# Four-chosen experts: two pairs' weights spread by TensorE, low weight parts made by GpSimd, chunk 1 prepared between the first units

## The chip, the core and the metric

The kernel runs on one core of a Trainium2 chip. The metric is the device time of one execution in microseconds (us). The core's engines run beside each other, each with its own order of instructions: TensorE (PE; its weight loads are PEld), VectorE (DVE), ScalarE (ACT), GpSimd (POOL) and SyncE (SP), which issues DMAs. They wait for each other through semaphores.

## The reference

A stack of eight blocks on x of 2048 tokens by 128 features: softmax attention, two-chosen experts, a selective scan, two-chosen experts again, linear attention, four-chosen experts, gated linear attention, and four-chosen experts again. The change is in the function for the four-chosen experts, which is built twice. Cut to what matters:

```python
def _gate(x_flat, gate_w, e_bias):
    scores = sigmoid(x_flat @ gate_w.T)                  # 16 experts in 4 groups
    scores_for_choice = scores + e_bias
    # the sum of the best 2 of a group rates it; the best 2 groups stay; of their experts the best 4
    topk_weight = scores at the 4 chosen; weight / (weight.sum + 1e-20) * 2.5
x = x + _L1_attn_a_ref(_layernorm(x), ...)
x = x + _L1_ffn_ref(_layernorm(x), ...)                  # four-chosen experts, first stage
x = x + _L1_attn_b_ref(_layernorm(x), ...)
x = x + _L1_ffn_ref(_layernorm(x), ...)                  # four-chosen experts, second stage
#   with, in _L1_ffn_ref:
g = einsum('th,eih->eti', x, gate_proj); u = einsum('th,eih->eti', x, up_proj)
expert_out = einsum('eti,ehi->eth', silu(g) * u, down_proj)
y = sum over the chosen experts of topk_weight * expert_out
out = y + (silu(x @ shared_gate_w.T) * (x @ shared_up_w.T)) @ shared_down_w.T
```

## The kernel before

`experts_top4` (line 1883) works on 4 chunks (NC_) of 512 tokens (CH), each of 4 tiles (TPC) of 128. Work is laid out transposed: features on the partitions, tokens in the columns. The 16 experts have a hidden width of 64, so two share the 128 partitions: 8 pairs. With the shared expert, unit 0, a chunk has 9 units (UNITS); units are numbered g = 9c + u over the chunks, 36 in all (LAST).

A unit goes through four steps. `up(g)` (line 1994) is six matmuls on TensorE into two PSUM banks, gate and up: products in float32r are made exact enough by splitting weights and rows into a high and a low part, three matmuls for each bank (`SplitRows.matmul`, lines 120 to 122). `silu(g)` (line 2058) on ScalarE makes the gate. `multiply(g)` (line 2103) on VectorE multiplies the gate with the routing weights, spread over the partitions (line 2110, increments `scaled`), and then with the up bank (line 2116, increments `hidden_done`). `down(g)` (line 2006) is four matmuls of 128 columns (eight records, as float32 takes two for each) that add into the bank DOWN over all units of a chunk; `add(c)` adds the bank to x. Three sets of buffers (SETS) let up(g+3) start when hidden(g) is done.

The high part of the weights is rounded by ScalarE (line 2083, four instructions for two pairs each), the low part is subtracted by VectorE (`cut_weights`, line 2130, after multiply(0)); `up` waits for it on line 2002. A chunk's rows are prepared by `stat_rows` and `norm_rows` on VectorE (lines 162 to 168 and 183) with GpSimd's `root` between them (line 177), `turn` on TensorE (line 192), `copy_turned` on ScalarE (lines 200 and 202) and `cut_rows` on VectorE (line 210). Routing is `score` (TensorE, line 1975, into bank DOWN for chunk 0, SCRATCH for others), `tanh` (ScalarE), and `rate_groups`, `rank_groups`, `find_best`, `select` and `weigh` on VectorE, 28 short instructions in a chain (lines 2143 to 2200). The weights are turned by `turn_probs` (line 1985) into bank SCRATCH and copied by `copy_probs` (line 2066) to probsT, 16 rows of 512. SyncE stores them to DRAM (line 1946) and then loads each expert's row back into 64 partitions, two loads for a pair, into a ring of six tiles (line 1953).

Order on the engines is written by hand. TensorE (lines 2021 to 2047): turn(0), score(0), up(0), turn_probs(0), up(1), up(2); then for each unit g: turn(1) and score(1) at g = 1, down(g), up(g+3); from chunk 1 on turn_probs at u = 7, the next turn at u = 8, score at u = 0. ScalarE: round the shared weight, copies of chunk 0, tanh(0), silu(0), the four roundings, copy_probs(0), silu(1) to silu(3), the copies of chunk 1, tanh(1). VectorE: routing of chunk 0, multiply(0), cut_weights, then stat_rows(1), norm_rows(1), cut_rows(1), and only then multiply(1); the routing of the next chunk is put behind multiply of units 1 to 5 (one part each), statistics, normalising and cutting of the chunk after it behind units 6, 7 and 8.

## Time and profile before

| | us |
|---|---|
| median of 3 runs | 1628.84 (1627.59 to 1629.21) |
| the profiled execution | 1628.38 |
| its span | 1626.7 |
| TensorE busy in the span | 1485.5 (91%) |
| VectorE busy in the span | 1360.6 (84%) |
| first four-chosen stage, about | 1321 to 1435 |
| second four-chosen stage, about | 1512 to 1625 |

The profile is of one execution. A timeline row has the start in us from the span's start, the busy time, the engine, the line of the kernel, the operation, output<-inputs, shapes and the number of instructions merged; in brackets the idle time before it and what released it. TensorE's granted clock is given as a share of 2.4 GHz.

### The profile page before, as it was taken

Reading aid. Unit: us, or ns where it says so; the run is one execution under the profiler, and the core shown is the slowest. Engines: PE = TensorE matmul, PEld = TensorE weight load, DVE = VectorE, ACT = ScalarE, POOL = GpSimd, SP = SyncE. Lnnn points to the kernel's source line nnn. Section 1 sums busy time; section 2 is a strip of 40 time slices with the busy share of each in tenths; the row PEclk is TensorE's granted clock in tenths of the full one; section 3 lists DMA queues with packets and bytes.
Section 4 is the critical chain, followed back from the end, with each engine's and each line's share of the span. In section 5 each row is a group of like instructions: output and inputs, shape, how many; then the busy total and the mean of one; then the engine's idle time right before and its main releaser. Section 6 shows DMA issues by size and latency. Waiting matters only on the chain. (4 is left out here: it accounts for less than half of the span.)

```text
span 1626.7 us, 27667 instructions
## 1 busy us (share of the span) xinstructions
PE 1485.5 (91%) x10314; PEld 771.6 (47%) x10314; DVE 1360.6 (84%) x2455; ACT 936.1 (58%) x1751; POOL 295.8 (18%) x352
## 2 busy tenths in 40 slices
PE   7999999999999999799997898877999869989698
PEld 2122222222222222488862333324888748869587
DVE  7999999999999997476747999997767658787686
ACT  3189999999999999532236666653322332222232
POOL 4200000000000000000016878872000200020000
PEclk8599999999999999899999999999999979999799
DMA  3341100000000011000002222120000002300123
GB/s 108 118 141 31 34 31 25 25 25 25 25 24 25 32 42 33 1 1 1 1 1 72 73 66 69 66 71 4 1 1 1 1 19 88 106 1 1 53 84 101
DMA packets 41329, 66.15 MB, mean 41 GB/s; under 512 B 11444, under 2 KB 18661, under 8 KB 40490
## 3 DMA queue, kind: packets, MB, share of 16 engines
q1 hardware_dynamic: 41194, 64.37, 12.9%
q8 instruction: 82, 1.34, 0.3%
q14 instruction: 53, 0.43, 0.1%
HBM read 56.68 MB, written 6.75 MB: 39 GB/s over the span
## 5 line engine op out<-in xcount | busy, mean ns | idle before, releaser
L874 DVE TENSOR_REDUCE row_max<-ps 128x1 f32<-128x1024 f32 x512 | 585.1, 1213 | 16.5 <-PE ps L659 16.2
L780 ACT ACTIVATE probs<-ps 128x512 f32<-128x512 f32 x944 | 505.6, 596 | 57.1 <-PE ps L674 40.6
L659 PE MATMUL ps<-k_stack,q_stack 48*128 48x512 bf16 x1024 | 323.7, 402 | 8.4 <-DMA k_stack<-parts 2.7
L600 PE MATMUL ps<-probs,v_head 128*16 128x256 f32 (+1 forms) x3800 | 313.5, 402 | 6.3 <-issue 6.3
L674 PE MATMUL ps<-q_stack,k_stack 51*128 51x512 bf16 x944 | 286.9, 385 | 3.4 <-DMA q_stack<-max_dram 2.7
L1400 PE MATMUL ps<-s_hc,ident 128*128 128x512 f32 x256 | 139.0, 628 | 47.9 <-DVE s_hc L1673 42.8
L1053 ACT ACTIVATE x_gate<-ps 128x512 f32<-128x512 f32 x128 | 76.4, 598 | 184.5 <-PE ps L122 184.4
L659 PEld LDWEIGHTS ps<-k_stack,q_stack 48*128 48x128 bf16 x1024 | 60.1, 95 | 253.7 <-DVE row_max L874 234.6
L1325 POOL TENSOR_TENSOR s_dbx<-s_dx,s_b_rows 128x512 f32<-128x512 f32 x128 | 159.4, 1271 | 35.2 <-DVE s_h L1664 34.7
L1664 DVE TENSOR_TENSOR_SCAN s_h<-ps,s_state,s_dbx 128x512 f32<-128x512 f32 x128 | 156.8, 1266 | 4.5 <-POOL s_dbx L1325 2.8
L600 PEld LDWEIGHTS ps<-probs,v_head 128*16 128x16 f32 x3800 | 62.6, 94 | 201.5 <-issue 100.8
L1555 ACT ACTIVATE ps<-s_delta,s_a_neg 128x512 f32<-128x512 f32 x128 | 87.3, 689 | 77.7 <-DVE s_h L1664 76.7
L1090 DVE TENSOR_TENSOR x_hidden<-x_gate,ps 128x512 f32<-128x512 f32 x128 | 87.1, 686 | 53.4 <-PE ps L122 42.8
L1022 PE MATMUL ps<-w_w,x_hidden 128*128 128x128 f32 x1024 | 124.9, 275 | 0.0
L1022 PEld LDWEIGHTS ps<-w_w,x_hidden 128*128 128x128 f32 x1024 | 122.7, 192 | 3.6
L2063 ACT ACTIVATE y_gate<-ps 128x512 f32<-128x512 f32 (+1 forms) x72 | 43.0, 597 | 118.9 <-PE ps L122 118.9
L120 PE MATMUL ps<-x_x_high,x_w_high 128*128 128x512 f32 x256 | 107.6, 420 | 1.0 <-DVE x_hidden L1090 1.0
L122 PE MATMUL ps<-x_x_low,x_w_high 128*128 128x512 f32 x256 | 102.3, 400 | 0.0
L1400 PEld LDWEIGHTS ps<-s_hc,ident 128*128 128x128 f32 x256 | 45.6, 195 | 117.1 <-DVE s_hc L1673 87.6
L121 PE MATMUL ps<-x_x_high,x_w_low 128*128 128x512 f32 x256 | 101.1, 395 | 0.0
L1101 DVE SCALAR_TENSOR_TENSOR x_res<-ps,x_probs,x_res 128x128 f32<-128x128 f32 x256 | 72.1, 344 | 34.7 <-PE ps L1022 34.4
L1673 DVE TENSOR_TENSOR s_hc<-s_h,ps 128x512 f32<-128x512 f32 x128 | 80.9, 670 | 1.0 <-PE ps L1400 1.0
(346 smaller groups left out, 1953.6 us busy)
## 6 DMA issues: line engine op xcount, KB each, us to landing
s_b_rows<-s_b_dram SPq DMA_DIRECT2D x64, 256.0 KB, 3.2
y_spread<-y_probs_dram SPq DMA_DIRECT2D x128, 128.0 KB, 3.0
q_stack<-q_parts_dram SPq DMA_DIRECT2D x30, 96.0 KB
k_stack<-k_parts_dram SPq DMA_DIRECT2D x30, 96.0 KB
w_w<-w_dram SPq DMA_DIRECT2D x1, 2048.0 KB, 8.3
q_stack<-q_parts_dram SPq DMA_DIRECT2D x30, 64.0 KB
k_stack<-k_parts_dram SPq DMA_DIRECT2D x30, 64.0 KB
o_dram<-o_sb SPq DMA_DIRECT2D x60, 32.0 KB
```

Of the source, the lines that this page charges most:

```text
L120: nc.tensor.matmul(bank, self.w_high[:, u, cols], self.x_high[:, chunk], start=True, stop=False)
L121: nc.tensor.matmul(bank, self.w_low[:, u, cols], self.x_high[:, chunk], start=False, stop=False)
L122: return nc.tensor.matmul(bank, self.w_high[:, u, cols], self.x_low[:, chunk], start=False, stop=True)
L600: last = nc.tensor.matmul(core.ps[32 * c:32 * c + VROWS, O_BANK, cut], v_head[buf][:, kt, :], probs[:, m % RING, c * CH:(c + 1) * CH][:, cut],
L659: last = nc.tensor.matmul(core.ps[:, 2 * b + r, :], qst[buf][0:KROWS, u * P:(u + 1) * P], kst[buf][0:KROWS, key:key + CH], start=True, sto ...
L674: nc.tensor.matmul(core.ps[:, S_BANK + n % S_RING, :], kst[buf][HALF:ROWS, kt * P:(kt + 1) * P], qst[buf][HALF:ROWS, c * CH:(c + 1) * CH], ...
L780: nc.scalar.activation(probs[:, us % RING, c * CH:(c + 1) * CH], core.ps[:, S_BANK + n % S_RING, :], ACT.Exp).then_inc(exp_done, 1)
L874: nc.vector.tensor_reduce(mx[:, head % 2, u, b:b + 1], core.ps[:, 2 * b:2 * b + 2, :], mybir.AxisListType.XY, ALU.max).then_inc(max_done, 1)
L1022: last = nc.tensor.matmul(core.ps[:, DOWN + n % 2, k * P:(k + 1) * P], hidden[n % 2][:, half, k * P:(k + 1) * P], w["w3"][:, e, half, :], ...
L1325: nc.gpsimd.tensor_tensor(dbx[u % RING][:], dx[c % 2][d][:], b_rows[g % RING][:], ALU.mult).then_inc(dbx_done, 1)
L1400: nc.tensor.matmul(core.ps[:, Y_BANK + d, :], core.ident[:], hc[d][:], start=s == 0, stop=s == DS - 1).then_inc(summed, 1)
L1664: nc.vector.tensor_tensor_scan(out=h[g % 2][:, d, :], data0=core.ps[:, A_BANKS[d], :], data1=dbx[u % RING][:], initial=state[:, s, d:d + 1 ...
```

## The change

Four things in `experts_top4`, for chunk 0 alone or for the preparation of chunk 1:

- The routing weights of pairs 0 and 1 of chunk 0 no longer come through DRAM. `spread_rows` has TensorE multiply probsT with a column of the identity, repeated 64 times, once for each half of the partitions, into bank SCRATCH (pair 0) and bank DOWN (pair 1); multiply(1) and multiply(2) read them there. SyncE loads pairs 2 to 7. down(0), which writes DOWN, waits until multiply(2) has read it.
- The low parts of the 8 pairs' weights are subtracted by GpSimd; ScalarE rounds two groups ahead of silu(0) and two behind it.
- TensorE's order becomes turn(0), score(0), up(0), up(1), up(2), turn_probs(0), the two spreads, up(3), down(0), turn(1), down(1), up(4), score(1), down(2) and so on. ScalarE copies probs after silu(2), the turned rows of chunk 1 after silu(3), and makes tanh(1) after silu(4).
- VectorE: statistics of chunk 1 follow multiply(0), normalising follows multiply(1), the cut multiply(2); the routing of chunk 1 follows units 4 (two parts), 5 (two parts) and 6. Later chunks are as before.

```diff
--- before.py
+++ after.py
@@ -1887,7 +1887,7 @@
     PAIRS = E1 // 2
     UNITS = PAIRS + 1
     PG = E1 // GROUPS
-    SETS, P_RING = 3, 6
+    SETS, P_RING, BY_PE = 3, 6, 2
     DOWN, SCRATCH = 2 * SETS, 2 * SETS + 1
     LAST = NC_ * UNITS
     with ExitStack() as ctx:
@@ -1919,6 +1919,8 @@
         scored = core.sem(f"{tag}_scored")
         tanh_done = core.sem(f"{tag}_tanh")
         probs_ready = core.sem(f"{tag}_probs_ready")
+        rows_spread = core.sem(f"{tag}_rows_spread")
+        w_rest = core.sem(f"{tag}_w_rest")
         probs_turned = core.sem(f"{tag}_probs_turned")
         probs_copied = core.sem(f"{tag}_probs_copied")
         probs_stored = core.sem(f"{tag}_probs_stored")
@@ -1945,7 +1947,7 @@
                 sp.wait_ge(probs_copied, c + 1)
                 sp.dma_start(pd[c], probsT[:]).then_inc(probs_stored, 16)
                 sp.wait_ge(probs_stored, 16 * (c + 1))
-                for pair in range(PAIRS):
+                for pair in range(0 if c else BY_PE, PAIRS):
                     m = c * PAIRS + pair
                     if m >= P_RING:
                         sp.wait_ge(scaled, m - P_RING + 1)
@@ -1962,6 +1964,12 @@
         def _(pool):
             if following:
                 following.set_power(pool)
+            for i in range(PAIRS // 2):
+                pool.wait_ge(cut.w_rounded, i + 2)
+                nc.gpsimd.tensor_tensor(cut.w_low[:, 1 + 2 * i:3 + 2 * i, :],
+                                        w["w_up1"][:, 2 * i:2 * i + 2, :, :].rearrange("p u k d -> p u (k d)"),
+                                        cut.w_high[:, 1 + 2 * i:3 + 2 * i, :].bitcast(F32),
+                                        ALU.subtract).then_inc(w_rest, 1)
             ln.root(pool, 1)
             for g in range(LAST):
                 c, u = g // UNITS, g % UNITS
@@ -1999,7 +2007,10 @@
                 if u == 0:
                     pe.wait_ge(ln.x_cut, c + 1)
                 if c == 0:
-                    pe.wait_ge(cut.w_cut, 1 + (u + 1) // 2)
+                    if u:
+                        pe.wait_ge(w_rest, (u + 1) // 2)
+                    else:
+                        pe.wait_ge(cut.w_cut, 1)
                 for k in range(2):
                     cut.matmul(core.ps[:, 2 * (g % SETS) + k, :], u, slice(k * P, (k + 1) * P), cols).then_inc(up_done, 1)
 
@@ -2007,7 +2018,7 @@
                 c, u = g // UNITS, g % UNITS
                 pe.wait_ge(hidden_done, g + 1)
                 if u == 0 and c == 0:
-                    pe.wait_ge(tanh_done, 1)
+                    pe.wait_ge(scaled, BY_PE)
                 elif u == 0:
                     pe.wait_ge(added, c)
                 for k in range(TPC):
@@ -2018,18 +2029,34 @@
                                             stop=u == UNITS - 1 and k == TPC - 1)
                 last.then_inc(down_done, 1)
 
+            def spread_rows(pair):
+                if pair == 0:
+                    pe.wait_ge(probs_copied, 1)
+                else:
+                    pe.wait_ge(tanh_done, 1)
+                for i in range(2):
+                    e = 2 * pair + i
+                    last = nc.tensor.matmul(core.ps[i * I1:(i + 1) * I1, (SCRATCH, DOWN)[pair], :],
+                                            core.ident[0:E1, e:e + 1].to_broadcast([E1, I1]), probsT[:],
+                                            start=True, stop=True)
+                last.then_inc(rows_spread, 1)
+
             core.loaded(pe, "gate1", "w_down1", "sh_down")
             ln.turn(pe, 0)
             score(0)
-            up(0)
+            for g in range(SETS):
+                up(g)
             turn_probs(0)
-            for g in range(1, SETS):
-                up(g)
+            for pair in range(BY_PE):
+                spread_rows(pair)
             for g in range(LAST):
                 c, u = g // UNITS, g % UNITS
+                if g == 0:
+                    up(SETS)
                 if g == 1:
-                    pe.wait_ge(probs_copied, 1)
+                    pe.wait_ge(scaled, 1)
                     ln.turn(pe, 1)
+                if g == 2:
                     score(1)
                 if u == 7 and c + 1 < NC_:
                     turn_probs(c + 1)
@@ -2043,7 +2070,7 @@
                         pe.wait_ge(probs_copied, NC_)
                     following.turn(pe, u - 5)
                 down(g)
-                if g + SETS < LAST:
+                if g and g + SETS < LAST:
                     up(g + SETS)
 
         @block.scalar
@@ -2075,17 +2102,25 @@
             ln.copy_turned(act, 0)
             core.act_line.after(act, nc.scalar.activation(warm[:], core.one[:], ACT.Silu))
             tanh(0)
+
+            def round_weights(i):
+                nc.scalar.copy(cut.w_high[:, 1 + 2 * i:3 + 2 * i, :],
+                               w["w_up1"][:, 2 * i:2 * i + 2, :, :].rearrange("p u k d -> p u (k d)")).then_inc(
+                                   cut.w_rounded, 1)
+
+            round_weights(0)
+            round_weights(1)
             for g in range(LAST):
                 c, u = g // UNITS, g % UNITS
                 silu(g)
                 if g == 0:
-                    for i in range(PAIRS // 2):
-                        nc.scalar.copy(cut.w_high[:, 1 + 2 * i:3 + 2 * i, :],
-                                       w["w_up1"][:, 2 * i:2 * i + 2, :, :].rearrange("p u k d -> p u (k d)")).then_inc(
-                                           cut.w_rounded, 1)
+                    round_weights(2)
+                    round_weights(3)
+                if g == SETS - 1:
                     copy_probs(0)
                 if g == SETS:
                     ln.copy_turned(act, 1)
+                if g == SETS + 1:
                     tanh(1)
                 if u == 0 and c:
                     copy_probs(c)
@@ -2106,9 +2141,13 @@
                 dve.wait_ge(gate_done, g + 1)
                 if u:
                     m = c * PAIRS + u - 1
-                    dve.wait_ge(spread_loaded[m % P_RING], 32 * (m // P_RING + 1))
-                    nc.vector.tensor_tensor(gate[g % SETS][:], gate[g % SETS][:], spread[m % P_RING][:],
-                                            ALU.mult).then_inc(scaled, 1)
+                    if m < BY_PE:
+                        dve.wait_ge(rows_spread, m + 1)
+                        weights = core.ps[:, (SCRATCH, DOWN)[m], :]
+                    else:
+                        dve.wait_ge(spread_loaded[m % P_RING], 32 * (m // P_RING + (m % P_RING >= BY_PE)))
+                        weights = spread[m % P_RING][:]
+                    nc.vector.tensor_tensor(gate[g % SETS][:], gate[g % SETS][:], weights, ALU.mult).then_inc(scaled, 1)
                     dve.wait_ge(scaled, m + 1)
                 dve.wait_ge(up_done, 2 * g + 2)
                 if g >= SETS:
@@ -2126,14 +2165,6 @@
                 dve.wait_ge(cut.w_rounded, 1)
                 nc.vector.tensor_tensor(cut.w_low[:, 0, :], w["sh_up"][:].rearrange("p k d -> p (k d)"),
                                         cut.w_high[:, 0, :].bitcast(F32), ALU.subtract).then_inc(cut.w_cut, 1)
-
-            def cut_weights():
-                for i in range(PAIRS // 2):
-                    dve.wait_ge(cut.w_rounded, i + 2)
-                    nc.vector.tensor_tensor(cut.w_low[:, 1 + 2 * i:3 + 2 * i, :],
-                                            w["w_up1"][:, 2 * i:2 * i + 2, :, :].rearrange("p u k d -> p u (k d)"),
-                                            cut.w_high[:, 1 + 2 * i:3 + 2 * i, :].bitcast(F32),
-                                            ALU.subtract).then_inc(cut.w_cut, 1)
 
             def rate_groups(c):
                 part = slice(c * TPC, (c + 1) * TPC)
@@ -2210,17 +2241,28 @@
             select(0)
             weigh(0)
             multiply(0)
-            cut_weights()
             ln.stat_rows(dve, 1)
-            ln.norm_rows(dve, 1)
-            ln.cut_rows(dve, 1)
             for g in range(LAST):
                 c, u = g // UNITS, g % UNITS
                 if g:
                     multiply(g)
                 if u == 0 and c:
                     add(c - 1)
-                if c + 1 < NC_:
+                if c == 0:
+                    if u == 1:
+                        ln.norm_rows(dve, 1)
+                    elif u == 2:
+                        ln.cut_rows(dve, 1)
+                    elif u == 4:
+                        rate_groups(1)
+                        rank_groups(1)
+                    elif u == 5:
+                        find_best(1)
+                        select(1)
+                    elif u == 6:
+                        dve.wait_ge(probs_ready, 1)
+                        weigh(1)
+                elif c + 1 < NC_:
                     if u == 1:
                         rate_groups(c + 1)
                     elif u == 2:
```

## Rows read from the trace of the kernel before

**Rows 1.** The page, busy time of each engine.

```profile
PE 1485.5 (91%) x10314; PEld 771.6 (47%) x10314; DVE 1360.6 (84%) x2455; ACT 936.1 (58%) x1751; POOL 295.8 (18%) x352
```

**Rows 2.** Windows, first stage: length, busy (instructions) by engine, clock, DMA share, GB/s.

```profile
1321.00:1336.00 15.00, 8.94 (x27) 6.43 (x28) 10.61 (x45) 6.93 (x13) 0.09 (x1) 0.50 0.02 4
1336.00:1343.00 7.00, 5.09 (x26) 3.75 (x25) 2.77 (x13) 2.35 (x5) 1.01 (x1) 0.98 0.47 133
1343.00:1350.30 7.30, 7.23 (x29) 6.68 (x30) 5.91 (x21) 0.82 (x2) 0.00 (x0) 0.53 0.53 158
1350.30:1367.40 17.10, 17.02 (x109) 14.87 (x108) 14.53 (x45) 5.87 (x11) 1.39 (x1) 1.00 0.11 29
```

**Rows 3.** Timeline, all engines, 1325 to 1328.

```profile
1325.27 0.77 PE L120 MATMUL ps<-y_x_high,y_w_high 128*128 128x512 f32 x1
...
1325.89 0.19 DVE L2143 TENSOR_SCALAR y_scores<-y_scores 128x64 f32<-128x64 f32 x1 [1.68 <-ACT y_scores L2054]
...
1327.43 2.16 ACT L2083 CAST y_w_high<-w_w_up 128x512 fp32r<-128x512 f32 x4
...
1327.55 0.63 PE L122 MATMUL ps<-y_x_low,y_w_high 128*128 128x512 f32 x1
```

**Rows 4.** Timeline, all engines, 1332 to 1337.

```profile
1332.33 0.22 DVE L2200 TENSOR_TENSOR y_probs<-y_gt,y_total 128x64 f32<-128x64 f32 x1
...
1332.61 1.02 PE L1990 MATMUL ps<-ident,y_probs 128*16 128x128 f32 x4 [4.43 <-DVE y_probs L2200]
...
1333.07 2.48 DVE L2133 TENSOR_TENSOR y_w_low<-w_w_up,y_w_high 128x512 fp32r<-128x512 f32 x4
...
1333.67 0.57 ACT L2070 COPY y_probsT<-ps 16x512 f32<-16x512 f32 x1 [4.08 <-PE ps L1990]
...
1333.80 0.80 PE L120 MATMUL ps<-y_x_high,y_w_high 128*128 128x512 f32 x1 [0.17 <-DVE y_w_low L2133]
...
1336.94 11.63 SPq L1953 DMA_DIRECT2D y_spread<-y_probs_dram  x16
```

**Rows 5.** Timeline, the preparation of chunk 1, 1336 to 1343.

```profile
1336.79 0.17 DVE L168 TENSOR_SCALAR ln_m_veps<-ln_m_mv 128x4 f32<-128x4 f32 x1
...
1337.11 1.01 POOL L177 TENSOR_TENSOR ln_m_rstd<-ln_m_veps,ln_m_power 128x4 f32<-128x4 f32 x1 [16.01 <-DVE ln_m_veps L168]
...
1338.15 1.12 DVE L183 TENSOR_SCALAR xn<-x_res,ln_m_mv,ln_m_rstd 128x128 f32<-128x128 f32 x4 [1.19 <-POOL ln_m_rstd L177]
...
1340.49 0.60 PE L192 MATMUL ps<-ident,xn 128*128 128x128 f32 x4
...
1342.23 0.69 DVE L210 TENSOR_TENSOR y_x_low<-ps,y_x_high 128x512 fp32r<-128x512 f32 x1 [2.97 <-ACT xnT L202]
...
1342.84 0.68 DVE L2110 TENSOR_TENSOR y_gate<-y_gate,y_spread 128x512 f32<-128x512 f32 x1
```

**Rows 6.** Timeline, VectorE and TensorE in full stride, and down(9).

```profile
1354.64 0.69 DVE L2110 TENSOR_TENSOR y_gate<-y_gate,y_spread 128x512 f32<-128x512 f32 x1
...
1354.89 0.48 PE L120 MATMUL ps<-y_x_high,y_w_high 128*128 128x512 f32 x1
...
1355.98 0.22 DVE L2196 TENSOR_TENSOR y_gt<-y_scores,y_sel 128x64 f32<-128x64 f32 x1
...
1357.17 0.48 PE L120 MATMUL ps<-y_x_high,y_w_high 128*128 128x512 f32 x1
...
1367.40 1.13 PE L2015 MATMUL ps<-w_sh_down,y_hidden 64*128 64x128 f32 x8
```

**Rows 7.** Lines and timeline elsewhere: prices of operations like the new ones.

```profile
L1325 POOL TENSOR_TENSOR s_dbx<-s_dx,s_b_rows 128x512 f32<-128x512 f32 x128 | 159.4, 1271 | 35.2 <-DVE s_h L1664 34.7
...
1359.93 1.39 POOL L177 TENSOR_TENSOR ln_m_rstd<-ln_m_veps,ln_m_power 128x4 f32<-128x4 f32 x1 [21.82 <-DVE ln_m_veps L168]
...
1436.45 2.81 PE L2382 MATMUL ps<-xnT,w_W_in 128*128 128x512 f32 x6 [1.52 <-PEq L1893]
...
499.63 0.63 PE L600 MATMUL ps<-probs,v_head 128*16 128x256 f32 x8
```

## The prediction

> **What bounds the kernel now.** I read the page first: TensorE is busy for 91% of the span [rows 1], so a gain has to come from a place where it is idle or slow. The table by windows over the first four-chosen stage shows such a place [rows 2]. In 1321 to 1336 TensorE is busy for 8.9 of 15 us, at a granted clock of 0.50 (1.2 GHz); in 1343 to 1350.3 it is busy all the time but at 0.53; from 1350.3 it is full, at 1.00 (2.4 GHz). The timeline says why. TensorE ends up(0) at 1328.0 and then waits until 1332.6 for the routing weights of chunk 0, because turn_probs(0) stands ahead of up(1) in its order; VectorE works on those weights without a pause from 1325.9 to 1332.55 [rows 3, 4]. The four weight subtractions follow (1333.1 to 1335.55), and up(1) waits for the first of them until 1333.8 [rows 4]. Then VectorE prepares the rows of chunk 1 before multiply(1): statistics to 1336.96, waiting for GpSimd's root, 1.12 us of normalising, and 2.97 us waiting for TensorE's turn and ScalarE's copies; the cut is at 1342.23, and multiply(1) starts at 1342.84 [rows 5]. From unit 4 on TensorE is the bound: 2.28 us a unit against 1.34 us of multiplying and 1.1 to 1.6 us of routing on VectorE [rows 6]. So the stage has a start set by VectorE's order and a long part set by TensorE. The yardstick is down(9), the first product of chunk 1, at 1367.40 [rows 6]: behind it both kernels issue the same work. The second four-chosen stage repeats these rows 191.3 us later, so what one stage gains counts twice.
>
> **Part by part.** *Low parts to GpSimd.* VectorE loses 4 instructions, 2.48 us [rows 4]. GpSimd gets 4 subtractions of 128x512; its tensor_tensor of that size takes 1.27 us [rows 7], 5.1 us in all. ScalarE now rounds two groups ahead of silu(0): it is free when tanh has released VectorE at 1325.9, and takes 0.54 us for each [rows 3], so the first low part exists at 1325.9 + 0.54 + 1.27 = 1327.7, before up(0) ends at 1328.0, and all four by 1331.5, ahead of the root for chunk 1 that is queued behind them. silu(0) moves by at most 0.1 us; nobody waits, since hidden(0) comes after the routing.
>
> *up(1), up(2) ahead of turn_probs(0).* They fill the idle 4.6 us. At the low clock each takes 2.56 us (six at 0.43) [rows 3] and up(2) ends at 1333.1, 0.5 us after the routing weights; if the clock rises on the way, at 1331 to 1332, and nothing is late. In the kernel before the clock rose at 1336, 3.4 us after TensorE took up steady work at 1332.6 [rows 2, 4]; here steady work starts at 1325.3, so I take a rise at about 1329 to 1332.
>
> *Weights of pairs 0 and 1 by TensorE.* Four loads of sixteen leave SyncE's queue; pair 2 is then the first, and its load, issued at about 1336.5, is in long before it is wanted. The store still goes ahead of it. In exchange: turn_probs at 1332.6, which takes 0.63 us to ScalarE's start at the full clock (1.06 at the low one [rows 4]), the copy 0.57 [rows 4], and two matmuls of 512 f32 columns with 64 output rows each. The nearest row: six records of 512 f32 columns, two to a matmul, in 2.81 us [rows 7], so 0.9 us for one. Whether the two halves of the partitions run together decides between 0.9 and 1.8 us. The row nearest to it is the value product of attention, four column blocks side by side: eight records (four matmuls) of 256 f32 columns in 0.63 us [rows 7], where four in turn would take 1.8 by the 0.9 for 512 columns; I take together. At the full clock the pair's weights are then ready at 1332.6 + 0.63 + 0.6 + 1.1 = 1334.95. At the low clock this is 1336.3, or 1338 with the halves in turn.
>
> The Trainium skill, "TensorEngine Tiling (Array Packing)", Key Properties, says that tiles run in parallel and that a change of tiling mode drains TensorE. The attention row agrees with the first half; no row here separates out a drain, and the sum has none.
>
> *Chunk 1 between the units.* VectorE: multiply(0) and statistics end at 1334.55; multiply(1) 1334.95 to 1336.3 (1.34 [rows 6]); normalising to 1337.4; the scaling of multiply(2) ends at 1338.05. There is one new wait: down(0) now waits for it, because its bank holds the weights of pair 1, and turn(1) is queued behind down(0). Meanwhile TensorE has done the second spread and up(3), to 1337.2, and idles 0.9. down(0) 1.06 (taken from a unit's share, 2.28 less six times 0.23, and a little more for the wait ahead of it [rows 6]), turn(1) 0.6, ScalarE's two copies 1.1 (1341.1 to 1342.2 [rows 5]): cut_rows(1) at 1340.9 instead of 1342.23 [rows 5], and multiply(1) and (2) are already done. That is the gain: two units of VectorE work (2.7) and the low parts (2.5) leave the stretch between the weights and this point.
>
> From there VectorE is the bound to the end of chunk 0, since routing for chunk 1 now lies in units 4 to 6: cut 0.6, multiply(3) to (8) 6 x 1.34 = 8.0, routing 6.6 (1325.89 to 1332.55 [rows 3, 4]), statistics and normalising of chunk 2 1.4 + 1.1 [rows 5], and 1.4 us for GpSimd's root beside a multiply [rows 7], partly covered: 0.1. Sum 17.8, multiply(8) ends at 1359. TensorE is not late: its five units from 1344 take 11.4. It has up(11) done at 1361.4 (down(8) waits for multiply(8), then turn(2) and up(11) at 2.3), score(2) 1.04, and down(9) starts at about 1362.3, against 1367.40: 5.1 us.
>
> Off this I take 0.8: 0.3 for GpSimd delayed beside VectorE and 0.5 for a clock that may be low over part of the spread. That leaves 4.3 a stage, 8.6 in all. The profiled execution took 1628.4 (span 1626.7 and 1.7 around it), 0.4 below the median of 1628.8; its sum is 1619.8, and on the median it is 1620.2.
>
> **What isn't shown before.** GpSimd streaming while VectorE reads two SBUF tensors: GpSimd's 4-column root takes 1.39 us beside the two-tensor multiply, where it takes 1.01 without it [rows 5, 7], so GpSimd yields and VectorE's 0.69 doesn't change. Bounds: nothing (as beside the scan, 1.27), up to each low part doubled (10 us), which puts the root 2 us late. Whether VectorE's chain of 28 small instructions slows, no row shows: from 0 to the whole 5.1 us, if the two took turns. I take 0, as VectorE's row says. The Trainium skill, "GPSIMD Engine Reference", Key points, states that the two engines contend where VectorE has two SBUF inputs or a two-port mode, which nearly all these 28 have; by that rule alone the gain could be nil, as in the port case below.
>
> **Rivals.** *The clock is low over the spread.* TensorE idles about 1 us ahead of turn_probs and 0.6 behind it. Before, an idle stretch of 2 us at 1341 was followed by the low clock [rows 2]; the gaps here are shorter. Price: turn 0.43 and matmuls 0.9 at least, queue 0.5 and later waits 0.5 besides: 1.3 to 2.3 us of the 5.1. Taking 2.3 and the 0.3 for GpSimd, 2.5 is left: 1623.8.
> *Port.* GpSimd's and VectorE's streams stretch each other on the routing chain: 2 to 3 us in each stage, 1.8 left: 1625.2. Its extreme, 5.1, is no change: 1628.8.
> *Slower.* The spread runs at the low clock and its halves in turn, 3.4 us each: pair 0 at 1338, pair 1 at 1341.3, multiply(2)'s scaling at 1342.1, up(3) at the low clock to 1343.9, down(0) and turn(1) 2.8, copies 1.1: the cut at 1347.9 instead of 1340.9, and down(9) 7.0 later than in the sum and 0.4 more for units still at the low clock, at 1369.7, 2.3 late: 1633.4. It decides where up(3), down(0), turn(1) and the copies (6.5 in all) behind pair 1's weights reach 1340.9 + 5.1: from 1339.5 on. Against it: eight attention records side by side.
> *It does not do it.* The starting wait merely changes its name: down(0)'s new wait, or VectorE's compressed chunk-1 routing, costs what was won. The sum has 4 us in hand before this holds: 1628.8.
>
> **How the numbers follow.** Forecast case 55% (1618.0 to 1622.5), low clock 20% (up to 1624.9), port 12% (1623 to 1628.8), not done 6%, slower 7%. The low end is 5.5 us a stage with everything free: 1617.5. The high end takes in the low clock and half of the port case: 1626.5. A difference under 0.2% (3.3 us) can't be told from none in this kernel. Faster by more: 55 + 19 + 5 = 79%; within: 13%; slower: 8%.
>
> **What would show it.** Right: up(1) at 1328 directly behind up(0); pair 0's scaling at about 1335; cut_rows(1) at about 1341; down(9) at about 1362; GpSimd's four rows near 1.3 us; granted clock 1.0 from about 1331. Wrong: pair weights after 1336 (clock, or halves in turn); routing weights later than 1332.6 after the stage's start at 1321 (port); VectorE idle in units 4 to 8 while TensorE works (then the sum of chunk 0 is wrong).

## The result, and the profile after

The changed kernel takes 1633.44 us (median of 7 runs, 1631.58 to 1636.14) against 1628.87 for the kernel before (7 runs); the ratio is 1.0032, with a 95% interval of 1.0023 to 1.0041. It is slower by 0.3%, where the forecast was 0.5% faster. The page after:

```profile
span 1634.4 us, 27691 instructions
...
PE 1494.0 (91%) x10330; PEld 775.1 (47%) x10330; DVE 1364.5 (83%) x2447; ACT 936.6 (57%) x1751; POOL 305.9 (19%) x360
```

The profiled execution took 1636.14 us, the longest of the seven. Its first four-chosen stage begins 3.0 us later than before (first turn 1324.31, before 1321.29), in code that is the same up to there; so I count from the stage's first turn.

The windows that answer to [rows 2], from the stage's first turn on, cut at the end of the routing before (11.3 us), near the start of down(0) before (16; it is 16.6), the cut of chunk 1 before (21) and after (28). The columns are the same: length, busy time and instructions of PE, PEld, DVE, ACT and POOL, granted clock, DMA share, GB/s.

```profile
1324.30:1335.60 11.30, 9.31 (x30) 7.13 (x30) 7.56 (x16) 6.81 (x13) 5.08 (x4) 0.62 0.01 1
1335.60:1340.30 4.70, 0.41 (x3) 0.26 (x4) 4.18 (x22) 0.00 (x0) 0.00 (x0) 0.93 0.00 0
1340.30:1345.30 5.00, 4.34 (x12) 0.99 (x10) 3.06 (x14) 0.57 (x1) 1.01 (x1) 0.50 0.12 39
1345.30:1352.30 7.00, 7.00 (x25) 5.74 (x26) 2.08 (x6) 1.67 (x3) 0.00 (x0) 0.50 0.59 198
1352.30:1374.30 22.00, 21.22 (x133) 18.55 (x133) 19.00 (x63) 6.88 (x13) 1.39 (x1) 0.98 0.11 34
```

TensorE fills the first stretch as planned, and near its end, at 1332.8, its clock rises to 2.4 GHz. Then it is idle: busy for 0.4 of 4.7 us. From 1340.3 to 1352.3 it is busy almost throughout, at a granted clock of 0.50 (1.2 GHz). The timeline of the routing, after, shows what the idle stretch waits for:

```profile
1329.40 0.19 DVE L2178 TENSOR_TENSOR y_hi<-y_choice 128x32 f32<-128x32 f32 x1
1329.43 5.08 POOL L1969 TENSOR_TENSOR y_w_low<-w_w_up,y_w_high 128x512 fp32r<-128x512 f32 x4 [5.32 <-ACT y_w_high L2107]
1329.51 1.28 DVE L2179 TENSOR_TENSOR y_lo<-y_choice 128x32 f32<-128x32 f32 x1
...
1330.83 1.20 DVE L2180 TENSOR_TENSOR y_g_best<-y_hi 128x16 f32<-128x16 f32 x1
...
1331.95 0.16 DVE L2181 TENSOR_TENSOR y_g_next<-y_hi 128x16 f32<-128x16 f32 x1
1332.03 1.26 DVE L2182 TENSOR_TENSOR y_g_low<-y_lo 128x16 f32<-128x16 f32 x1
...
1333.33 1.21 DVE L2183 TENSOR_TENSOR y_g_next<-y_g_next,y_g_low 128x16 f32<-128x16 f32 x1
...
1334.58 0.17 DVE L2184 TENSOR_TENSOR y_g_best<-y_g_best,y_g_next 128x16 f32<-128x16 f32 x1
```

GpSimd's four subtractions run from 1329.43 to 1334.51, 1.27 us each, as [rows 7] had said. Beside each, one short VectorE instruction takes 1.2 to 1.3 us; the same lines take 0.17 to 0.18 us in every other chunk. L2181, which begins together with GpSimd's third, slips through in 0.16. The first instruction that starts after GpSimd is done takes 0.17 again. The chain from its first step to the routing weights takes 10.9 us (1328.91 to 1339.83) where it took 6.7 [rows 3, 4]. What follows, after:

```profile
1339.61 0.22 DVE L2231 TENSOR_TENSOR y_probs<-y_gt,y_total 128x64 f32<-128x64 f32 x1
...
1339.89 1.02 PE L1998 MATMUL ps<-ident,y_probs 128*16 128x128 f32 x4 [5.11 <-DVE y_probs L2231]
...
1340.95 0.57 ACT L2097 COPY y_probsT<-ps 16x512 f32<-16x512 f32 x1 [6.22 <-PE ps L1998]
...
1341.58 3.68 PE L2039 MATMUL ps<-y_probsT,ident 16*64 16x512 f32 x8 [0.66 <-ACT y_probsT L2097]
...
1343.66 0.69 DVE L2150 TENSOR_TENSOR y_gate<-y_gate,ps 128x512 f32<-128x512 f32 x1 [1.84 <-PE ps L2039]
...
1348.04 2.07 PE L2026 MATMUL ps<-w_sh_down,y_hidden 64*128 64x128 f32 x8
...
1352.30 0.69 DVE L210 TENSOR_TENSOR y_x_low<-ps,y_x_high 128x512 fp32r<-128x512 f32 x1 [4.88 <-ACT xnT L202]
...
1374.08 1.13 PE L2026 MATMUL ps<-w_sh_down,y_hidden 64*128 64x128 f32 x8
```

turn_probs(0) comes 5.1 us after TensorE's last work and at the low clock; the two spreads take 3.68 us, down(0) 2.07, where 1.06 was expected. The cut of chunk 1 is at 1352.30, 28.0 us after the first turn (before 20.9 [rows 5]). From there to down(9) it is 21.8 us, where the sum had 21.4. The second stage repeats the first: down(9) 49.96 after its first turn, 46.10 before the change.

This table gives the marks of the first four-chosen stage of every kernel, in us after its first turn, from the timelines; in brackets the second stage where it differs by over 0.3. "x before" is the ratio of the times.

| kernel | routing weights begin | multiply(1) | cut of chunk 1 | down(9) | x before |
|---|---|---|---|---|---|
| before | 11.0 | 21.6 | 20.9 | 46.1 | 1 |
| after | 15.3 | 19.4 | 28.0 | 49.8 | 1.0032 |
| e1, before with GpSimd's low parts | 14.4 | 24.7 | 24.1 | 49.2 | 1.0034 |
| e2, after, low parts in VectorE's gaps | 11.1 | 13.8 | 21.2 | 42.8 | 0.9945 |
| e3, after, GpSimd's behind the routing | 11.0 | 18.4 (18.8) | 24.5 (24.8) | 45.9 (46.3) | 0.9985 |
| e4, after, GpSimd's in halves | 15.0 | 19.1 (18.7) | 27.7 (27.3) | 49.5 | 1.0028 |
| e5, e2 with turn(1) first | 11.1 | 13.8 | 18.9 | 41.3 | 0.9933 |
| e6, e2 with idle filled | 11.1 | 13.8 | 20.5 (21.2) | 41.9 (42.8) | 0.9944 |
| e7, e2 without the spread | 11.1 | 17.8 | 22.1 | 44.7 | 0.9985 |
| e8, e5 with half of up(3) early | 11.1 | 14.0 | 18.3 | 42.6 (40.3) | 0.9931 |
| e9, after with idle filled | 15.3 | 18.1 | 24.7 | 46.2 | 0.9991 |
| e10, before with the gaps used | 11.1 | 18.9 | 18.3 | 43.5 | 0.9963 |

### The profile page after: what moved, and what is told of

Same layout as the page of the kernel before. It is cut to its first block and busy times, and to the rows that moved or that the text cites. A ratio compares the mean times of both kernels' runs of the same rounds, so it can differ in the third digit from the quotient of the medians.

```text
span 1634.4 us, 27691 instructions
## 1 busy us (share of the span) xinstructions
PE 1494.0 (91%) x10330; PEld 775.1 (47%) x10330; DVE 1364.5 (83%) x2447; ACT 936.6 (57%) x1751; POOL 305.9 (19%) x360
## 5 line engine op out<-in xcount | busy, mean ns | idle before, releaser
L1090 DVE TENSOR_TENSOR x_hidden<-x_gate,ps 128x512 f32<-128x512 f32 x128 | 87.2, 686 | 53.3 <-PE ps L122 42.8
L508 POOL TENSOR_TENSOR neg_max_parts<-neg_maxT,by_one 128x32 bf16<-128x32 f32 x16 | 4.0, 251 | 418.5 <-DVE neg_maxT L867 418.5
```

## The experiments

The theory after the result had two parts: P, GpSimd's streaming holds up VectorE's routing instructions, and K, the wait that this makes lets TensorE's clock fall, which stretches all that follows. The rival C was that the order and the clock alone are to blame.

**e1_low_by_gpsimd.** One part of the change alone, in the kernel before.

```diff
         def _(pool):
+            for i in range(PAIRS // 2):
+                pool.wait_ge(cut.w_rounded, i + 2)
+                nc.gpsimd.tensor_tensor(cut.w_low[...], w["w_up1"][...], cut.w_high[...], ALU.subtract).then_inc(w_rest, 1)
             ln.root(pool, 1)
...
             multiply(0)
-            cut_weights()
```

> The kernel before with one thing changed: the four subtractions of the low weight parts are GpSimd's instead of VectorE's (TensorE's order, the DRAM way of the routing weights and the preparation of chunk 1 stay). Theory P (port: while GpSimd's tensor_tensor streams, a VectorE instruction with two SBUF inputs waits for its end): some four of the short routing instructions take 1.2 to 1.3 us instead of 0.2, the routing weights of chunk 0 come 4 us later after the stage's first turn (15.3 instead of 11.3), and with 2.5 us of VectorE work gone that was not on the path the time is 8 us above before, 1636.5. Rival C (the changed kernel lost its time only to the clock and the new order): the short instructions keep 0.2 us and the time is 1628.5.

Measured: 1634.51 us, ratio 1.0034 (1.0022 to 1.0046); the routing weights 3.3 us late, down(9) 3.1. Timeline:

```profile
1328.80 0.22 DVE L2174 TENSOR_TENSOR y_g_beats<-y_g_beats,y_g_ties 128x64 f32<-128x64 f32 x1
1328.82 4.99 POOL L1968 TENSOR_TENSOR y_w_low<-w_w_up,y_w_high 128x512 fp32r<-128x512 f32 x4 [7.09 <-ACT y_w_high L2093]
1329.06 0.22 DVE L2175 TENSOR_REDUCE y_g_rank<-y_g_beats 128x16 f32<-128x64 f32 x1
1329.32 0.87 DVE L2177 TENSOR_SCALAR y_g_rank<-y_g_rank 128x16 f32<-128x16 f32 x1
1330.22 1.24 DVE L2181 TENSOR_TENSOR y_tmp_scores<-y_choice,y_g_rank 128x64 f32<-128x64 f32 x1
1331.49 0.41 DVE L2186 MAX8 y_top<-y_tmp_scores 128x8 f32<-128x16 f32 x4
1331.93 0.74 DVE L2189 TENSOR_TENSOR y_gt<-y_tmp_scores,y_top 128x64 f32<-128x64 f32 x1
1332.60 1.29 DVE L2190 TENSOR_TENSOR y_eq<-y_tmp_scores,y_top 128x64 f32<-128x64 f32 x1
```

P holds, C falls: this one edit costs as much as the whole change. The last two lines show best that it is a wait for the end of GpSimd's instruction: L2189 begins midway through GpSimd's third, which ends at 1332.59, and takes 0.74 us; L2190 meets the fourth almost whole and takes 1.29. Here other routing instructions are hit, those that happen to lie beside GpSimd's, so it is not a property of single lines. The four MAX8 (0.41 us together) and the reduction, each with one SBUF input, keep their time; tensor_tensor with two SBUF inputs and tensor_scalar don't. Less was lost than I expected (5.5 us, not 8): the weights are 3.3 us late in each stage, not 4.

**e2_low_in_vector_gaps.** The changed kernel with that part given back to VectorE, half of it ahead of the routing.

```diff
-                nc.gpsimd.tensor_tensor(cut.w_low[...], ...)            # all four
+            round_weights(0)                                            # ScalarE, before copy_turned(0)
+            round_weights(1)                                            # ScalarE, before tanh(0)
             cut_shared()
+            cut_pairs(0)
             ln.cut_rows(dve, 0)
+            cut_pairs(1)
             rate_groups(0)
...
             ln.stat_rows(dve, 1)
+            cut_pairs(2)                                                # cut_pairs(3) behind multiply(2)
```

> The changed kernel with the low parts taken from GpSimd again: ScalarE rounds two groups before tanh(0), VectorE subtracts pairs 0 to 3 in its two idle stretches ahead of the routing, pairs 4 to 7 behind the statistics of chunk 1 and behind multiply(2). All else of the change stays. Theory P: the routing weights come 11.3 us after the first turn again. If port and clock cost 4.3 and 4.1 us a stage, as the traces read, only the first goes: each stage is 0.6 us shorter than before, 1627.5. If the clock was low only because TensorE waited 5 us for the late weights, it stays at 2.4 GHz now and the blind forecast's sum holds: down(9) 46.1 - 5 = 41 us after the first turn, 1619. Rival C: no better than the changed kernel, 1633.

Measured: 1620.19 us, ratio 0.9945 (0.9933 to 0.9957). Timeline:

```profile
1333.26 1.93 PE L2033 MATMUL ps<-y_probsT,ident 16*64 16x512 f32 x8 [0.66 <-ACT y_probsT L2091]
...
1334.46 0.69 DVE L2143 TENSOR_TENSOR y_gate<-y_gate,ps 128x512 f32<-128x512 f32 x1
...
1337.64 2.04 PE L2020 MATMUL ps<-w_sh_down,y_hidden 64*128 64x128 f32 x8
...
1341.87 0.69 DVE L210 TENSOR_TENSOR y_x_low<-ps,y_x_high 128x512 fp32r<-128x512 f32 x1 [3.05 <-ACT xnT L202]
```

The two spreads take 1.93 us at 2.4 GHz, pair 0's weights are read 2.5 us after the routing's end (the forecast's term was 2.4). With the low parts in this place the change gains 0.55%; e10 below shows how much of it is the place. Not all of the clock came back: down(0) still takes 2.04, so the cut is at 21.2 and not at the forecast's 19.6.

**e3_low_after_routing.** GpSimd keeps the subtractions but starts them when the routing is done.

```diff
         def _(pool):
+            pool.wait_ge(probs_ready, 1)
...
-            for g in range(SETS):
-                up(g)
-            turn_probs(0)
+            up(0)
+            turn_probs(0)
+            for g in range(1, SETS):
+                up(g)
```

> The changed kernel with GpSimd's four subtractions held back until the routing weights of chunk 0 are made, and turn_probs(0) ahead of up(1) as before the change. Theory P: no routing instruction is stretched, weights at 11.3; VectorE's next instructions (hidden product, statistics, product with a PSUM operand) have one SBUF input and keep their 0.69 us beside GpSimd. TensorE has up(1) and up(2) ahead of the spread, so pair 0's weights come at about 18.5 after the first turn and down(9) at about 46: 1629, same as before. If VectorE is slowed by any streaming of GpSimd, its 0.69 us instructions take up to 1.9 and the time is 1632 or more.

Measured: 1625.68 us, ratio 0.9985 (0.9976 to 0.9994). Timeline:

```profile
1332.16 4.99 POOL L1970 TENSOR_TENSOR y_w_low<-w_w_up,y_w_high 128x512 fp32r<-128x512 f32 x4 [11.60 <-DVE y_probs L2233]
1332.53 0.85 DVE L162 BATCH_NORM_STATS2 ln_m_stats<-x_res 128x6 f32<-128x128 f32 x4
1333.42 0.38 DVE L165 BATCH_NORM_AGGREGATE ln_m_mv<-ln_m_stats 128x2 f32<-128x6 f32 x4
...
1333.84 0.85 DVE L168 TENSOR_SCALAR ln_m_veps<-ln_m_mv 128x4 f32<-128x4 f32 x1
```

The statistics (0.85 and 0.38 for four each, as before) run beside GpSimd untouched; a tensor_scalar of 4 columns takes 0.85 instead of 0.17, to the end of GpSimd's second instruction (1334.66). The hidden product, with one SBUF and one PSUM tensor, kept its 0.67 us, but it had begun 0.2 us ahead of GpSimd, so it tests nothing. The trace of the kernel before does: in the selective scan 117 of the 128 instructions of this line began while GpSimd still had 0.15 us or more of a 128x512 tensor_tensor before it, and none was stretched (shortest, median and longest in ns):

```profile
L1673 DVE TENSOR_TENSOR s_hc<-s_h,ps x128: 656/668/690, 871.5 to 1116.6; 128x512 f32<-128x512 f32 x128
```

The marks came as expected, and the spread (1.93 us) and down(0) (1.13) ran at 2.4 GHz. The time was 3 us better than expected, and since the marks were not, the gain lies behind down(9): from there to down(27), the first product of the last chunk, the first stage takes 45.2 us against 46.0 before, and from the second stage's down(9) to the end it is 65.8 against 68.0. VectorE's waits for rows from DRAM in those stretches are 3.7 us in all, against 6.1 before.

**e4_halves.**

```diff
-            for i in range(PAIRS // 2):      # 512 columns each
+            for u in range(PAIRS):           # 256 columns each
```

> The changed kernel with GpSimd's four subtractions of 512 columns as eight of 256. Theory P: a VectorE instruction waits for the rest of one GpSimd instruction, so about eight routing instructions take 0.7 to 0.85 us where four took 1.25; the weights come at about the same time, 15.5 us after the first turn, and the time is that of the changed kernel, 1633.5. Rival (each meeting costs a fixed 1 us, whatever the size of GpSimd's instruction): eight instructions of 1.2 us, weights at 19.5, time 1641.

Measured: 1633.56 us, ratio 1.0028 (1.0017 to 1.0039), weights at 15.0. Timeline:

```profile
1327.19 5.65 POOL L1969 TENSOR_TENSOR y_w_low<-w_w_up,y_w_high 128x256 fp32r<-128x256 f32 x8 [5.32 <-ACT y_w_high L2107]
1327.27 0.73 DVE L2179 TENSOR_TENSOR y_lo<-y_choice 128x32 f32<-128x32 f32 x1
...
1328.04 0.64 DVE L2180 TENSOR_TENSOR y_g_best<-y_hi 128x16 f32<-128x16 f32 x1
...
1331.46 0.77 DVE L2191 TENSOR_TENSOR y_g_ties<-y_g_best 128x64 f32<-128x64 f32 x1
...
1332.26 0.65 DVE L2194 TENSOR_TENSOR y_g_ties<-y_g_ties,w_earlier 128x64 f32<-128x64 f32 x1
```

GpSimd's eight take 0.7 us each, and eight VectorE instructions take 0.64 to 0.77 in this stage. The length of the wait goes with the length of GpSimd's instruction, and its end releases VectorE: theory P as stated, not a fixed price.

**e5_turn_first.**

```diff
                 if g == 0:
                     up(SETS)
-                if g == 1:
                     pe.wait_ge(scaled, 1)
                     ln.turn(pe, 1)
...
                 down(g)                      # down(0) now follows turn(1)
```

> e2_low_in_vector_gaps with TensorE's turn(1) moved ahead of down(0): turn(1) then waits only for the normalised rows and for multiply(1)'s reading of the bank, not for down(0) and through it for multiply(2). Theory W (the change's own new wait, down(0) behind the scaling of multiply(2), with turn(1) queued behind it, holds the rows of chunk 1 back, and VectorE paces the rest of chunk 0 from there): the cut of chunk 1's rows comes 2.0 us earlier in the stage (19.2 instead of 21.2 us after the first turn) and the time falls by 3 to 4, to 1616.5. Rival (from there on the loads of pair 2 or TensorE are late instead): no difference, 1620.

Measured: 1618.34 us, ratio 0.9933 (0.9921 to 0.9945). The cut is at 18.9, and down(9) 1.5 and 1.7 earlier in the two stages, a little under what was expected. In time it is 1.9 us, and the intervals of e2 and e5 overlap; the marks carry the reading, that turn(1) behind the change's new wait cost about 1.6 us a stage. Part of this may be the clock: behind the spread it was at 1.2 GHz for 3.4 us here (1338.4 to 1341.8) and for 6.9 in e2 (1335.6 to 1342.5), and no run holds it fixed.

**e6_warm.**

```diff
                 up(g)
+            keep_busy(SCRATCH, 4)
             turn_probs(0)
+            pe.wait_ge(tanh_done, 1)
+            keep_busy(DOWN, 2)
```

> e2_low_in_vector_gaps with six extra float32r matmuls of 512 columns on TensorE, whose results nobody reads: four ahead of turn_probs(0), two between it and the spread. In e2 TensorE stood at 2.4 GHz for turn_probs and the spread, and at 1.2 GHz from 1335.6 to 1342.3. Theory K (the idle gaps ahead of the spread bring the clock down): it stays at 2.4 GHz, up(3), down(0) and turn(1) take 1.4, 1.1 and 0.6 instead of 2.6, 2.0 and 1.1, the cut comes 1.5 us earlier and the time is 1617. Rival S (the spread with its 16 rows of weights does not hold the clock up, whatever stands ahead of it): the clock falls as before and the time is 1620 to 1621.

Measured: 1620.28 us, ratio 0.9944 (0.9929 to 0.9959): no gain. In the first stage TensorE waited 0.51 us ahead of turn_probs(0) and down(0) took 1.19 us (2.4 GHz); in the second it waited only 0.14 us and down(0) took 2.04 (1.2 GHz). Filling the last small gaps doesn't hold the clock, or not reliably. Neither K nor S is settled by it for this place.

**e7_all_through_dram.**

```diff
-    SETS, P_RING, BY_PE = 3, 6, 2
+    SETS, P_RING, BY_PE = 3, 6, 0
```

> e2_low_in_vector_gaps with the spread by TensorE undone: all eight pairs of chunk 0 come through DRAM, turn(1) waits for the copy of the weights, down(0) no longer for multiply(2). If the spread is worth its full 3.9 us of earlier weights for pair 0 (landing about 1338.4 against 1334.5 in e2), both stages lose that and the time is 1628. By the order of the waits I expect less: multiply(1) starts at 1338.4, the normalised rows are ready at 1341, turn(1) follows at once since nothing is queued ahead of it, and the cut comes at about 1342.6, 0.7 later than in e2: 1621.6.

Measured: 1626.70 us, ratio 0.9985 (0.9976 to 0.9993). multiply(1) comes 4.0 us later than in e2 and the cut 0.9, as expected, but down(9) 1.9 and 1.7, and the whole 6.5 us, so the expected 1621.6 was wrong. Of the 2.9 us behind down(9), 1.6 are waits of VectorE for spread rows in the later chunks of the second stage; the other 1.3 I can't place.

```profile
DVE y_gate L2143 <- DMA y_spread<-y_probs_dram: 3.4, 2, 2.0
```

```profile
DVE y_gate L2143 <- DMA y_spread<-y_probs_dram: 1.8, 1, 1.8
```

The first line is e7's, the second e2's (us in total, times, longest). So TensorE's spread is worth about 6 us, 3.6 of them by down(9).

**e8_turn_first_half_up.**

```diff
             turn_probs(0)
+            up(SETS, (0,))                   # gate half of up(3)
...
                 if g == 0:
-                    up(SETS)
+                    up(SETS, (1,))
```

> e5_turn_first with the three matmuls of the gate half of up(3) moved between turn_probs(0) and the spread, where TensorE waits 0.66 us for ScalarE's copy. They take 0.70 us at 2.4 GHz, so the pairs' weights are 0.1 us later and up(3) ends 0.7 to 1.3 us earlier. Theory K: with the gap closed the clock holds more often, and down(0) and turn(1) are earlier: up to 1 us a stage below e5, 1614.5. Rival S: the same as e5.

Measured: 1617.96 us, ratio 0.9931 (0.9919 to 0.9943): with e5, the fastest kernels here. Down(9) is at 42.6 in one stage and 40.3 in the other, with the same instructions; the difference is the clock again: at 1.2 GHz from 1337.5 to 1344.3 in the first stage, at 2.4 all through this place in the second. Timeline of the first stage:

```profile
1335.17 1.93 PE L2033 MATMUL ps<-y_probsT,ident 16*64 16x512 f32 x8
...
1337.04 0.50 PE L120 MATMUL ps<-y_x_high,y_w_high 128*128 128x512 f32 x1
...
1337.71 0.63 PE L122 MATMUL ps<-y_x_low,y_w_high 128*128 128x512 f32 x1
...
1339.55 2.04 PE L2020 MATMUL ps<-w_sh_down,y_hidden 64*128 64x128 f32 x8 [0.21 <-DVE y_gate L2143]
```

**e9_after_filled.** The changed kernel as it is, with TensorE kept at work through the wait.

```diff
                 up(g)
+            keep_busy(SCRATCH, 20)           # 512 columns each, results unread
             turn_probs(0)
```

> The changed kernel itself, GpSimd's subtractions where they are, with 20 extra float32r matmuls of 512 columns (results unread) ahead of turn_probs(0), where TensorE idles 5.1 us. It separates the clock from the late weights. Theory K: the idle brings the clock down to 1.2 GHz; filled, turn_probs and the spread run at 2.4 GHz, pair 0's weights come 2.75 us after the routing's last step (as in e2) instead of 4.05, the cut of chunk 1 at 25.5 us after the first turn instead of 28.0 and down(9) at 47.1 instead of 49.8; the weights themselves stay at 15.3. Time 5 us under the changed kernel, 1628.5. Rival (the clock is low for another reason, the spread with its 16 rows): spread 3.7 us again, 1633.5.

Measured: 1627.53 us, ratio 0.9991 (0.9981 to 1.0001). Timeline:

```profile
1331.10 4.70 PE L2046 MATMUL ps<-y_x_high,y_w_high 128*128 128x512 f32 x20
...
1336.51 0.60 PE L1998 MATMUL ps<-ident,y_probs 128*16 128x128 f32 x4 [0.71 <-DVE y_probs L2236]
...
1337.78 2.11 PE L2039 MATMUL ps<-y_probsT,ident 16*64 16x512 f32 x8 [0.67 <-ACT y_probsT L2102]
```

The routing weights come as late as in the changed kernel, yet turn_probs takes 0.60 us, the spread 2.11, the cut is at 24.7, and the time is 5.9 us lower. K holds for the idle of 5.1 us, the rival falls. The clock still fell behind the spread, but for 3.4 us (1339.4 to 1342.8) and not for 13.6 (1339.7 to 1353.3). It also splits the bill: 5.9 us for the clock (3.6 and 3.8 at the two down(9)), and 7.3 from here to e2 (6.7 and 7.5 by the ratios). The 7.3 are for the late weights (4.2 us a stage) less what e2 pays for its own low clock, which lasts 6.9 us there, so the late weights by themselves may cost more; no run shows that apart.

**e10_before_with_gaps.** The kernel before with the low parts as in e2 (pairs 4 to 7 behind multiply(0)) and up(1), up(2) ahead of turn_probs(0); nothing else.

```diff
-            up(0)
+            for g in range(SETS):
+                up(g)
             turn_probs(0)
-            for g in range(1, SETS):
-                up(g)
...
+            cut_weights((0,))
             ln.cut_rows(dve, 0)
+            cut_weights((1,))
             rate_groups(0)
```

> The kernel before with only this: ScalarE rounds two groups and VectorE subtracts pairs 0 to 3 in VectorE's idle stretches ahead of the routing, pairs 4 to 7 behind multiply(0), and TensorE does up(1) and up(2) ahead of turn_probs(0). Nothing is spread by TensorE, nothing of chunk 1 is moved between units. VectorE prepares chunk 1 some 1.2 us earlier and TensorE is free for turn(1) sooner: cut of chunk 1 at 19 instead of 20.9, multiply(1) at 19.6, down(9) at 44 instead of 46.1: 1624.5. If this part is worth nothing by itself, 1628.8; if it is the whole gain of e2, 1620.

Measured: 1623.94 us, ratio 0.9963 (0.9949 to 0.9977), down(9) at 43.5, close to what was expected. This reordering alone has more than half of e2's gain.

## Why the prediction was wrong

**What bounds the kernel.** Right in the main, with two corrections. The first is on the start. It is not VectorE's order alone that sets it: in the kernel before the normalised rows of chunk 1 are ready at 1339.3, and turn(1) begins at 1340.49 [rows 5], because TensorE works without a pause through up(1), up(2), down(0) and up(3) ahead of it. In e1 VectorE has 2.5 us less to do between the weights and the cut, and the way takes 9.7 us instead of 9.9; in e10, where up(1) and up(2) are out of it and VectorE has half of the subtractions, 7.3.

The second is on the yardstick. The changed kernel is 7.5 us late at down(9), both stages together, but only 4.6 slower by the medians (5.2 by the ratio; the profiled execution is 7.8 longer, 3.0 of it ahead of the first stage). It wins 2.7 back behind down(9). VectorE's waits for rows from DRAM in the later chunks are 6.1 us before and 3.8 after; most of the difference is in the second stage (before, then after):

```profile
DVE y_gate L2110 <- DMA y_spread<-y_probs_dram: 4.0, 2, 2.2
```

```profile
DVE y_gate L2150 <- DMA y_spread<-y_probs_dram: 2.1, 2, 1.9
```

e2 gains 6.5 at down(9) and 2.7 behind it, 9.2 in all, against 9.0 by the ratio. The forecast had no term for the stretch behind down(9); why the waits are shorter there no run tests.

**Low parts to GpSimd.** This step failed first. The time of GpSimd's own work was right (1.27 us each). The step "so GpSimd yields and VectorE's 0.69 doesn't change" read [rows 5, 7] wrongly: a root of 4 columns beside a multiply of 512 shows what happens when VectorE has begun first. With GpSimd in the lead it is VectorE that waits, to the end of GpSimd's instruction. I took 0 from a range of 0 to 5.1 us; it was 4.3 in each stage, by the sum of the four stretched instructions (1.28 + 1.20 + 1.26 + 1.21, less 0.7 for their own time). The sentence on the Trainium skill ("GPSIMD Engine Reference", Key points) had the right rule, and the traces agree with it: the instructions hit are those with two SBUF inputs (1.19 to 1.32 us) and the tensor_scalar (0.85 and 0.87), the ones with a PSUM operand are not (L1673 above). I should have let it weigh more. The count of the chain was off too: 33 instructions by the trace, not 28, and 21 of them read two SBUF tensors.

The trace of before could have settled it ahead of the change, in a place that none of my rows came from, the gated linear attention:

```profile
1443.62 1.89 POOL L2353 TENSOR_TENSOR g_span<-g_f 128x1024 f32<-128x1024 f32 x1 [4.84 <-DVE g_f L2577]
...
1444.49 2.10 DVE L2590 TENSOR_TENSOR g_qd<-g_q_raw,g_f 128x1024 f32<-128x1024 f32 x1 [0.95 <-ACT g_q_raw L2524]
...
1448.15 1.23 DVE L2590 TENSOR_TENSOR g_qd<-g_q_raw,g_f 128x1024 f32<-128x1024 f32 x1 [0.36 <-ACT g_q_raw L2524]
```

The first product of two SBUF tensors starts while GpSimd has 1.02 us to go and takes 2.10; the second, which meets only the last 0.03 us of one, takes 1.23.

**up(1), up(2) early.** Right: up(1) followed up(0) without a gap worth naming, the clock rose 4.5 us after up(0) began (1328.3 to 1332.8), and by e10 this part, with the gaps, is worth 0.37%.

**The weights by TensorE.** The halves run together, as taken: two pairs in 1.93 us at 2.4 GHz and 3.68 at 1.2, so 0.97 for a pair. At the low clock a pair takes 1.84, and that is what happened, not for the gaps of 1 us and 0.6 that I weighed but for one of 5.1, which the late weights had made. This is the second step that failed: the sum took off 0.5 us a stage for the clock, and by the marks it was 4.1 (1.4 more to pair 0's weights, 2.7 more from there to the cut), of which filling the idle stretch in e9 gave back 3.6 and 3.8. The two costs were rivals in my list, to be paid one or the other. They were one chain.

**Chunk 1 between the units.** Mostly right. At full clock the way from pair 0's weights to the cut takes 6.0 us (e3: 18.4 to 24.5), in the sum 5.95; at the low clock 8.6. From the cut to down(9) 21.8 against 21.4. The new wait of down(0) was in the sum, and by e5 taking turn(1) out from behind it gives up to 1.6 us more.

**The slower rival** was given 7% with the low clock and the halves in turn. Its first half was right, its second was not, and that its price, 1633.4, is the measured time is chance: it had down(9) 2.3 us late in each stage, and it was 3.7 and 3.9. The port rival, at 12%, had 2 to 3 us where 4.3 were lost and kept the clock out. The time lies where both meet: the 5.1 of the sum, less 4.3 and 4.1, is 3.3 us lost a stage, and 0.4 more behind the cut makes 3.7. That e2 takes 1620.2, the forecast's number, is in part chance: its weights are in time, but its clock is low for part of the start, so it gains 3.3 and 3.2 at down(9) and not 4.3, and the 2.7 behind down(9) makes up for it.

**Open.** What decides whether and for how long the clock falls just behind the spread. It was at 1.2 GHz for 6.9 us in both stages of e2, for 3.4 in both of e5, for 3.4 and 6.8 in e6, for 6.8 and not at all in e8, and not at all in e3: in e6 and e8 the same code shows both in its two stages.

## What to carry to other kernels

Before moving a tensor_tensor to GpSimd "beside" VectorE, look at what VectorE does meanwhile: if it is a latency chain of short instructions with two SBUF inputs, each of them can wait out a whole GpSimd instruction, and the chain pays most of GpSimd's time (4.3 of 5.1 us here, 3.3 of 5.0 in e1). Put such work into idle stretches of VectorE itself, or beside its instructions with a PSUM operand, as the scan does. Look through the whole trace for a place where the two engines already meet that way. And when two costs stand in a list as rivals, ask whether one brings on the other: here a late result made an idle TensorE, and the idle TensorE a slow one.

## What the runs showed of the hardware

- A VectorE tensor_tensor with two SBUF inputs that meets a running GpSimd tensor_tensor takes as long as that needs to end: 1.19 to 1.32 us instead of 0.17 to 0.22 beside 512 columns, 0.60 to 0.78 beside 256, 0.74 where it began midway. A tensor_scalar with one SBUF input waits too (0.85 and 0.87 instead of 0.17). MAX8 and a reduction (e1), statistics (e3), and a product with a PSUM operand (the scan, 0.66 to 0.69) don't. GpSimd's own time stays at about 1.27 us.
- Two float32 matmuls of 512 columns with 16 rows and 64 output rows each, for the two halves of the partitions, take 0.97 us together at 2.4 GHz (0.94 for one of full width, from the 2.81 us for three in [rows 7]) and 1.84 at 1.2 GHz.
- After 5.1 us of idling in the changed kernel TensorE ran at 1.2 GHz for 12 us (1340.3 to 1352.3) although one gap of 0.66 us was its only rest; 3.7 us of this were the spread, with 16 rows of weights. With the idle stretch filled (e9) the low clock lasted 3.4 us.
